# An attention loop rebuilt on full PSUM banks, its transposes moved to VectorE, and a one-hot operand read from PSUM

## What is computed

```python
# causal attention, C = 128, 16 heads of D = 8, T = 1024
k, q, v = split(x @ W_kqv.T)              # q and k get rope and an rms norm per head
scores = einsum('bhtd,bhsd->bhts', q, k) / sqrt(D)      # masked where s > t
y = einsum('bhts,bhsd->bhtd', softmax(scores), v)
x_term = y @ W_proj.T

# routed attention, four routes: top 128 rows as queries, top 64 rows as keys
q_top, q_idx = top_k(q_logits, 128); queries = x[q_idx]
kv_top, kv_idx = top_k(kv_logits, 64); key_values = x[kv_idx]
```

## Time and profile before

| what | value |
|---|---|
| time, median of 3 runs | 814.76 us (814.21 to 816.13) |
| the profiled execution: its time, and its span in the profile | 813.59 us, 811.8 us |
| mean granted TensorE clock | 0.892 |
| busy: PE, DVE, ACT, POOL | 641.5, 459.0, 441.7, 336.2 us |
| the attention loop (first to last exponential) | 170.8 to 309.0 us |

### The profile page before, as it was taken

One profiled execution on the slowest core, in us unless ns is written; L12 is line 12 of the kernel. 1 busy time (PEld: TensorE's weight loads), 2 busy tenths in 40 slices (PEclk: granted clock), 3 DMA queues, 4 the chain that ended last, 5 costly groups with the idle time before them and its releaser, 6 DMA issues. The chain is left out here.

```text
span 811.8 us, 13446 instructions
## 1 busy us (share of the span) xinstructions
PE 641.5 (79%) x4710; PEld 468.1 (58%) x4710; DVE 459.0 (57%) x1401; ACT 441.7 (54%) x847; POOL 336.2 (41%) x422
## 2 busy tenths in 40 slices
PE   6879777479999998049877599999729758999990
PEld 3757574222222224036567589999628747999980
DVE  7894859931111115985747545556556783555572
ACT  5565534579999995536544444444424373444440
POOL 1173343203332221256150657765431046677553
PEclk9689999569999999559998789999959967999996
DMA  8220000668000000002000576667330028666654
GB/s 327 95 73 35 1 2 0 207 213 305 6 2 1 2 1 1 1 4 104 1 1 8 148 252 217 214 190 203 110 103 1 1 63 291 209 217 194 192 162 161
DMA packets 36470, 87.60 MB, mean 108 GB/s; under 512 B 5169, under 2 KB 20145, under 8 KB 35377
## 3 DMA queue, kind: packets, MB, share of 16 engines
q1 hardware_dynamic: 31280, 76.13, 28.5%
q0 software_dynamic: 5120, 10.58, 4.6%
HBM read 69.75 MB, written 16.94 MB: 107 GB/s over the span
## 5 line engine op out<-in xcount | busy, mean ns | idle before, releaser
L1959 PE MATMUL ps<-arena 128*128 128x256 f32 (+1 forms) x768 | 156.8, 356 | 2.3 <-issue 1.2
L1505 ACT ACTIVATE arena<-ps,arena 128x256 f32<-128x256 f32 (+1 forms) x192 | 84.1, 438 | 129.1 <-issue 76.5
L1959 PEld LDWEIGHTS ps<-arena 128*128 128x128 f32 x768 | 129.9, 196 | 19.0 <-issue 3.4
L1450 ACT ACTIVATE arena<-ps 128x1024 f32<-128x1024 f32 (+2 forms) x160 | 135.8, 957 | 4.0 <-PE ps L1854 2.6
L975 DVE SCALAR_TENSOR_TENSOR arena<-ps,arena 128x256 f32<-128x256 f32 (+1 forms) x192 | 84.3, 440 | 82.3 <-ACT arena L1505 80.4
L611 POOL DMA_INDIRECT yd<-arena,wqk x80 | 78.6, 983 | 68.5 <-DVE arena L997 57.5
L575 POOL DMA_INDIRECT arena<-xs,wqk x80 | 77.6, 970 | 31.4 <-issue 15.2
L563 POOL TENSOR_SCALAR_AFFINE_SELECT arena<-arena 128x512 f32<-128x512 f32 x64 | 40.6, 635 | 111.8 <-ACT arena L1450 111.8
L1871 PE MATMUL ps<-arena 128*32 128x512 f32 (+3 forms) x768 | 83.3, 506 | 2.7 <-DVE arena L1208 1.6
L1970 PE MATMUL ps<-arena 128*128 128x128 f32 x640 | 79.5, 275 | 2.0 <-DVE arena L997 2.0
L1970 PEld LDWEIGHTS ps<-arena 128*128 128x128 f32 x640 | 75.2, 192 | 2.5 <-issue 2.4
(11 more groups left out here) (297 smaller groups left out, 1184.6 us busy)
## 6 DMA issues: line engine op xcount, KB each, us to landing
arena<-in_wall SPq DMA_DIRECT2D x48, 836.0 KB, 4.6
arena<-slots SPq DMA_DIRECT2D x2, 2048.0 KB, 7.2
arena<-scr_q SPq DMA_DIRECT2D x8, 512.0 KB, 6.6
arena<-scr_k SPq DMA_DIRECT2D x8, 512.0 KB, 7.7
arena<-yd SPq DMA_DIRECT2D x8, 512.0 KB, 5.5
xs<-Xn SPq DMA_DIRECT2D x8, 260.0 KB, 5.2
scr_q<-arena SPq DMA_DIRECT2D x4, 384.0 KB, 4.4
scr_k<-arena SPq DMA_DIRECT2D x4, 384.0 KB, 4.0
```

Of the source, the lines that this page charges most:

```text
L1450: nc.scalar.activation(dst, src, ACT.Exp, scale=AD ** -0.5).then_inc(sem("exp", i), 1)
L1505: nc.scalar.activation(sl[:, k % 3, 0:rows], ps[:, k % 3, 0:rows], ACT.Silu, bias=raw[:, slot, EW_BA + f:EW_BA + f + 1]).then_inc(sem("sil ...
L1959: ins = mm(ps[:, bank, 0:rows], raw[:, slot, w + P * f:w + P * (f + 1)], xTt[:, j % 2, 0:rows], start=True, stop=True)
```

## The change

- **Exponentials on full banks.** `ORDER` has ten steps. Tiles of 384 and 128 columns are joined in one step and share a bank (kt 1 with 3, kt 5 with 7); tiles of 256 columns put two heads in a bank. Every exponential covers two full banks (`FILL = 2`), 18 to a group, 144 in all. TensorE's order goes by fills: scores of fill k+3, then the PV of the steps whose last fill is k-1. P is a ring of twelve banks. The last step of a group is an unmasked tile.
- **Transposes on VectorE.** A finished unit is transposed in blocks of 32 x 32 by VectorE straight from PSUM (`yq`), then reciprocals and multiplication into `yn`, where four groups of heads fill the 32 columns of a block. After the fourth group a second block transpose makes YT. TensorE's `back`, the transposes of Y and ScalarE's copies go away. The rows of W_proj are permuted on the host to match.
- **Chunks projected in the loop.** Chunks 0, 1 and 2 are projected (into bank 6), added and their statistics taken inside the loop, after units 6, 8 and 14; chunk 3 at its end (bank 7).
- **The gather.** One more TensorE matmul writes the ramp to PSUM bank 6, and VectorE's comparisons read it there. The key one-hots of tiles 4, 9 and 14 are made by VectorE in one comparison each, and GpSimd and ScalarE make 13.

```diff
-        ORDER = ((0, 0), (1, 0), (0, 1), (1, 1), (0, 2), (1, 2), (0, 3), (1, 3), (1, 7), (1, 4), (1, 6), (1, 5))
+        ORDER = ((0, (0,)), (0, (1, 3)), (1, (0,)), (1, (1,)), (0, (2,)), (1, (6,)), (1, (4,)), (1, (2,)), (1, (5, 7)), (1, (3,)))
...
+        FILL, RING = 2, 3 * HG
+        SCORE_FILLS = 6 // FILL
+        FREED = [sum(n <= FILL * k + FILL - 1 - RING for n in FIRST_BANK) for k in range(NFILL)]
+        ADD_AT = [QC * NHG - 2, QC * NHG, UNITS - 2, UNITS - 1]
+        PROJECT_AFTER = [min(ENDS[u] + 3, len(STEPS) - 1) for u in ADD_AT[:-1]]
+        AP_BANK = [6 + u % 2 for u in ADD_AT]
...
# ScalarE
+                for k in range(NFILL):
+                    act.wait_ge(*at("sT", i, k + 1))
+                    if FREED[k]:
+                        act.wait_ge(*at("pvs", i, FREED[k]))
+                    n0, bank = FILL * k % RING, FILL * (k % SCORE_FILLS)
+                    nc.scalar.activation(Pa[:, n0:n0 + FILL, :], ps[:, bank:bank + FILL, :], ACT.Exp, scale=AD ** -0.5
+                                         ).then_inc(sem("exp", i), 1)
...
# VectorE, per unit
-                    nc.vector.tensor_copy(yT[:, u % 2, :], ps[:, 6 + u % 2, :]).then_inc(sem("yT", i), 1)
+                    nc.vector.transpose(yq[:, u % 2, :], ps[:, 6 + u % 2, :]).then_inc(sem("yq", i), 1)
...
+                    if hg == NHG - 1:
+                        link(ins)
+                        c = QC * b + qc
+                        nc.vector.transpose(YT[:, HALF * c:HALF * (c + 1)], yn[:, qc, :]).then_inc(sem("YT", i), 1)
+                    if u in ADD_AT:
+                        add_projected(ADD_AT.index(u))
...
# TensorE
+                def attended(c):
+                    pe.wait_ge(*at("YT", i, c + 1))
+                    pe.wait_ge(*at("yq", i, ADD_AT[c] + 1))
...
+                for k in range(SCORE_FILLS):
+                    scores(k)
+                for k in range(NFILL):
+                    if k + SCORE_FILLS < NFILL:
+                        scores(k + SCORE_FILLS)
+                    for s_ in range(len(STEPS)):
+                        if LAST_FILL[s_] == k - 1:
+                            attend(s_)
...
# the gather
+KEYS_DVE = (4, 9, 14)
+                mm(ps[:, 6, 0:P], ident, iota1, start=True, stop=True)
-                        iota1.unsqueeze(1).broadcast_to([P, G, NQ]),
+                        ps[:, 6, 0:P].unsqueeze(1).broadcast_to([P, G, NQ]),
```

More of the change, by code:

```diff
@@ L117 @@
 by_act = lambda t: t % 2 == 1
+KEYS_DVE = (4, 9, 14)
+KEYS_ACT = [t for t in range(NT) if t not in KEYS_DVE]
 SIGNALS = {
@@ L351, in build @@
[L351 to L354, removed]
+        ORDER = ((0, (0,)), (0, (1, 3)), (1, (0,)), (1, (1,)), (0, (2,)), (1, (6,)), (1, (4,)), (1, (2,)), (1, (5, 7)), (1, (3,)))
+        assert sorted((qc, kt) for qc, kts in ORDER for kt in kts) == [(qc, kt) for qc in range(QC) for kt in range(4 * qc + 4)]
@@ L355, in build @@
+        DIAG = [sum(masked(m) for m in range(n)) for n in range(len(STEPS) + 1)]
         ENDS = [n + 1 for n, x in enumerate(STEPS) if x[4]]
         UNIT = [sum(x[4] for x in STEPS[:n]) for n in range(len(STEPS) + 1)]
+        UNITS = B * NHG * QC
+        ADD_AT = [QC * NHG - 2, QC * NHG, UNITS - 2, UNITS - 1]
+        PROJECT_AFTER = [min(ENDS[u] + 3, len(STEPS) - 1) for u in ADD_AT[:-1]]
+        AP_BANK = [6 + u % 2 for u in ADD_AT]
+        assert ENDS[ADD_AT[0]] < ENDS[ADD_AT[0] + 1] and UNIT[-1] == UNITS
@@ L1665, in ffn @@
                         pe.wait_ge(*at("S", i, t + 1))
-                        pe.wait_ge(*at("Sk", i, t + 1))
+                        pe.wait_ge(*at("Sk", i, sum(m <= t for m in KEYS_ACT)))
                         for part in range(2):
@@ L1869, in pv @@
-                    for j in range(HG):
-                        h = HG * hg + j
-                        ins = mm(ps[32 * j:32 * j + 32, 6 + u % 2, q0:HALF], Va[:, TB * b + kt, VW * h:VW * h + 32],
-                                 Pa[:, s_ % 3, j, 0:HALF - q0], start=(kt == 0), stop=last_)
+                    if 0 in kts and u >= 2:
+                        pe.wait_ge(*at("yq", i, u - 1))
+                    if 0 in kts and u - 2 in ADD_AT:
+                        pe.wait_ge(*x_of(i + 1, ADD_AT.index(u - 2)))
@@ new lines, in pv @@
+                    where = {(j, kt): (FIRST_BANK[s_] % RING + x, col)
+                             for x, (m, pieces) in enumerate(BANKS[FIRST_BANK[s_]:FIRST_BANK[s_] + HG]) if m == s_
+                             for j, kt, col in pieces}
+                    for kt in kts:
+                        for j in range(HG):
+                            h = HG * hg + j
+                            n, col = where[j, kt]
+                            ins = mm(ps[32 * j:32 * j + 32, 6 + u % 2, first_query(qc, kt):HALF], Va[:, TB * b + kt, VW * h:VW * h + 32],
+                                     Pa[:, n, col:col + span(qc, kt)], start=(kt == 0), stop=last_ and kt == kts[-1])
@@ L1881, in attn @@
-                scores(0)
-                scores(1)
-                for s_ in range(len(STEPS)):
-                    if s_ + 2 < len(STEPS):
-                        scores(s_ + 2)
-                    pv(s_)
-                    if s_ and STEPS[s_ - 1][4]:
-                        back(UNIT[s_] - 1)
-                back(UNIT[-1] - 1)
-                for c in range(NC):
-                    pe.wait_ge(*at("Y", i, NHG * QC * (c // 2 + 1)))
-                    for t in range(4):
-                        ins = nc.tensor.transpose(ps[:, c, P * t:P * (t + 1)], Y[:, 4 * c + t, :], ident)
-                    ins.then_inc(sem("YTp", i), 1)
```

188 lines of the change are left out of this document (100 added, 88 removed).

## The result

The changed kernel takes **793.7 us** (median of 4 runs, 791.5 to 796.4) beside 814.5 for the kernel before: ratio 0.9744, 95% interval 0.971 to 0.9778. Timed again on another chip, in six runs, it took 797.3 (795.0 to 801.5) beside 813.4: 0.9815 (0.9783 to 0.9846). That 813.4 is the median of ten runs of the kernel before; an eleventh, of 2,133.9 us, was in a slow state and is left out. The two intervals don't overlap: the same two kernels differ more from one chip or session to the next than within one. Both put the gain clear of zero, and the first alone clear of 2%. Predicted were 797.1 and a range of 793.0 to 803.5; the first timing lies 0.7 us inside its lower end, the second on the forecast. The profiled execution took 796.42 us, with a span of 794.5.

What follows compares the result with a forecast made beforehand. ScalarE's exponentials were taken to set the loop's length. Gains of 4.9 (loop), 6.4 (end) and 6.4 (gather), 17.7 in all, took the profiled 813.6 to 795.9, plus 1.2 for the median: 797.1 us, range 793.0 to 803.5.

Steps and rivals of the forecast that it cites:

- The loop: Attention loop: full-bank exponentials and fewer ScalarE waits gain 4.9 us, bounds 0.3 and 6, giving a loop of 133.5.
- Merging: Attention loop: 144 exponentials instead of 160 over the same columns bring 0.3 to 0.5 us.
- The waits behind the start: Attention loop: ScalarE waits 0.6 us per group, 4.8 in eight groups, behind the transposes of `back`; these go.
- The start: Start of the attention loop: 1.4 us of waiting kept, for TensorE's lower clock.
- nothing is late: Loop order followed: scores arrive in time at each step; projections cost 0 to 0.2 us three times, 0.3 taken.
- Rival A: Attention loop: TensorE falls behind at double steps and projections, 0.6 us a group; 801.7 us, chance 17%.
- The end: From the last exponential to L726: 10.5 us instead of 16.9, gain 6.4, bounds 5 and 7.5.
- VectorE's start: End of the attention: VectorE begins 1.27 us after the last exponential, behind the last PV of 512 columns.
- The gather: Two routed stages: ramp in PSUM and three key one-hots on VectorE gain 6.4 us, 3.4 in the first, 3.0 in the second.
- Rival B: Gather: VectorE and GpSimd still hold each other up, VectorE needs 18 us instead of 16; 807.5 us, chance 8%.
- C: Attention loop: scores queued behind a masked PV wait for GpSimd's select, 0.28 us per masked tile; 815.0 us, chance 4%.
- D: Nothing moves: loop waits stay, transposes twice as slow, gather unchanged; 813 to 816 us, chance 2%.

Runs made afterwards that it cites:

- `back` kept: The changed kernel with transposes back added behind each unit, their result unused: loop 133.5 us beside 133.1.
- gather alone: The kernel before with only the gather's edits (ramp from PSUM, three key one-hots on VectorE): 805.4 us beside 813.4, ratio 0.9905.
- both runs with one of the two edits: The changed kernel with keys moved but ramp in SBUF (VectorE busy all 17.1 us of the first gather), and with ramp in PSUM but keys kept (gather 16.4 us).

## Why the prediction was right

- **The loop: 4.9 predicted, 5.2 found**, with errors that cancel. Merging brought 1.0 instead of 0.3 to 0.5, since the fixed part is 0.06 us and not 0.03 (nor 0.25, which by the prediction's own 0.605 and 0.915 should have been 0.30). The waits behind the start were 3.8 us and not 4.8: the exponentials cost 133.1 in all, not 132.1. That `back` made them was right in the main, 3.2 of the 3.8, but only in the order that it stood in; in the new one it costs nothing, and the prediction took the one neighbour in TensorE's queue for the whole cause. The start was to keep its 1.4 and fell from 1.3 to 0.5. Working through the order by hand ("nothing is late") held but for the projections: two of them cost 0.25 each, 0.5 in all, beside 0.3. So 1.0 + 3.8 + 0.9 - 0.5 took the place of 0.3 + 4.8 - 0.3 + 0.1. Rival A fell.
- **The end: 6.4 predicted, 6.2 found**, in a profile where the clock was 1.00 throughout (0.90 in the kernel before); where it was 0.86, 4.6. The block transpose, which no row of before showed, takes 0.72 beside 0.69 taken from the copy. Of the terms, VectorE's start was too early (1.27, found 1.85), since chunk 2's projection stands ahead of the last PV; the last copy of XT came at 8.0 instead of 7.4. From there to L753 it was 2.8 instead of 3.06.
- **The gather: 6.4 predicted, 8.5 found.** VectorE at 0.61, GpSimd unhindered and TensorE as the next bound all came as predicted. The 0.72 us that the prediction counted for a tile don't follow from its "13 per 2 us" (that gives 0.62), but were right: 11.4 for sixteen. The size of the first (3.4, found 5.5) was the clock. I counted 3.3 us at the lower level, and this execution had none. Where a run had it, the gain was 2.8 (`back` kept, clock 0.79) and 3.8 (gather alone, 0.89). The second gave 3.0, as predicted. Rival B fell: VectorE with one SBUF input doesn't hold GpSimd up, as the Trainium skill has it (SBUF — State Buffer, Who interferes with whom), and both runs with one of the two edits agree. B's price was wrong too: with the hold-up left in, the moved keys made the gather 1.8 us shorter, where B counted 2 longer.
- **The total.** 17.7 were predicted and the medians fell by 20.8 and 16.1. That the sum lies between is partly luck: the stretches gave 19.8, and the unchanged rest took some of it back. The 793.7 of the first timing lies below the forecast's own 794.5 to 799.5, where the prediction had put 4%.
- **Rivals C and D** fell: GpSimd's select takes 0.634 us as before, nothing broke in the loop's order.

## What to carry to other kernels

When a queue keeps its consumer waiting, what stands in front of the late work may be a cause only together with the order that it stands in: leave it out of the old order and put it into the new one before you credit either. Price back-to-back instructions by the ends of their records, not by durations. An operand that doesn't change and that VectorE reads beside a busy GpSimd belongs in PSUM, for one matmul. Where a stage begins after TensorE has idled, read its granted clock before you price it, and judge an edit of one or two microseconds by its stretch of the trace.

## What the runs showed of the hardware

- Code that is the same took 464.5 to 471.3 us over fourteen profiles (the rest), and the start 43.1 to 48.7, with TensorE's granted clock on different levels. From 30 to 40 us it was 0.74 in the changed kernel and 0.50 in its second profile, whose start is 4.2 us longer:

```profile
30.00:40.00 10.00, 8.47 (x76) 7.53 (x73) 8.19 (x39) 2.56 (x4) 0.39 (x2) 0.74 0.01 2
```

```profile
30.00:40.00 10.00, 9.42 (x59) 9.20 (x59) 6.47 (x33) 3.49 (x4) 0.00 (x0) 0.50 0.01 2
```

- Thirteen idle matmuls ahead of the second gather (3.2 and 1.6 us, while TensorE waited anyway) raised its clock from 0.80 to 1.00 and saved 1.8 us.
- An exponential from PSUM costs 0.917 us for 1,024 fp32 columns, 0.703 for 768 and 0.490 for 512, where they follow one another without a wait: some 0.06 us whatever the length.
- VectorE's block transpose of 512 fp32 columns takes 0.72 us from PSUM and 0.71 from SBUF.
- GpSimd's subtraction of 256 fp32 columns costs 0.58 us beside a VectorE with one of its inputs in PSUM and 1.02 beside a VectorE with two inputs in SBUF, which is itself held to 1.07 instead of 0.62.
